# A fused attention kernel whose rotary query is turned by SBUF transfers instead of a second set of score products

## What is computed

```python
def _rotate_half(x):
    x1, x2 = jnp.split(x, 2, axis=-1)
    return jnp.concatenate([-x2, x1], axis=-1)
def _apply_rope(x, cos, sin):
    return x * cos[None, None] + _rotate_half(x) * sin[None, None]
...
h = _rmsnorm(hidden_states, ln1_w)
kv = _rmsnorm(kv_states, ln1_w)
q = (h @ Wq).reshape(bsz, q_len, NH, HD).transpose(0, 2, 1, 3)    # NH = 16, HD = 64
k = (kv @ Wk).reshape(bsz, k_len, NKV, HD).transpose(0, 2, 1, 3)  # NKV = 4
v = (kv @ Wv).reshape(bsz, k_len, NKV, HD).transpose(0, 2, 1, 3)
q = _apply_rope(q, cos_q, sin_q)
k = _apply_rope(k, cos_k, sin_k)
...
scores = jnp.einsum('bhqd,bhkd->bhqk', q, k) / math.sqrt(HD)
probs = jax.nn.softmax(scores + attention_mask, axis=-1)
attn = jnp.einsum('bhqk,bhkd->bhqd', probs, v) ... @ Wo
hidden = residual + attn
x = jax.nn.silu(x @ Wgate) * (x @ Wup) @ Wdown    # x = _rmsnorm(hidden, ln2_w)
```

## Time and profile before

| | us |
|---|---|
| median of 3 runs | 478.11 (475.93 to 478.21) |
| the profiled execution, its own time | 478.35 |
| its span | 476.5 |
| PE busy | 444.5 (93% of the span) |
| DVE busy | 373.0 (78%) |
| ACT busy | 297.7 (62%) |
| POOL busy | 272.9 (57%) |

### The profile page before, as it was taken

One profiled execution on the slowest core, in us unless ns is written; L12 is line 12 of the kernel. 1 busy time (PEld: TensorE's weight loads), 2 busy tenths in 40 slices (PEclk: granted clock), 3 DMA queues, 4 the chain that ended last, 5 costly groups with the idle time before them and its releaser, 6 DMA issues.

```text
span 476.5 us, 16997 instructions
## 1 busy us (share of the span) xinstructions
PE 444.5 (93%) x6888; PEld 352.7 (74%) x6888; DVE 373.0 (78%) x927; ACT 297.7 (62%) x726; POOL 272.9 (57%) x331
## 2 busy tenths in 40 slices
PE   5699999999999999999989888999999999999996
PEld 4367666767676776689878676798888888878776
DVE  5599888879898888968788987869687777868463
ACT  2377767768777877666873566565666657554351
POOL 6546796669978787965561556336453544541220
PEclk9799999999999999999999999999999999999999
DMA  8980000000000000000000000000000000000000
GB/s 289 229 276 3 2 3 1 3 3 1 3 4 3 1 4 2 3 1 2 1 1 3 2 1 3 2 12 3 12 3 1 14 3 13 1 14 3 14 1 22
DMA packets 12436, 11.54 MB, mean 24 GB/s; under 512 B 5192, under 2 KB 10312, under 8 KB 12360
## 3 DMA queue, kind: packets, MB, share of 16 engines
q1 hardware_dynamic: 11640, 9.01, 6.8%
q10 hardware_dynamic: 720, 1.45, 0.8%
HBM read 9.42 MB, written 1.05 MB: 22 GB/s over the span
## 4 chain that ended last, share of the span: by engine, by line
PE 66%; DVE 13%; issue 7%; ACT 6%; POOL 5%; DMA 1%; POOLq 0%; ACTq 0%; DVEq 0%
PE ps L474 7%; PE ps L456 5%; PE ps L488 5%; PE ps L626 5%; PE ps L766 5%; PE ps L642 5%; PE ps L664 4%; PE ps L464 3%; PE ps L540 2%; PE ps L553 2%; PE ps L619 2%; PE ps L414 2%; PE ps L634 2%; ACT shared L873 2%; PE ps L415 2%
## 5 line engine op out<-in xcount | busy, mean ns | idle before, releaser
L1355 DVE TENSOR_REDUCE negm<-ps 128x8 bf16<-128x512 f32 x96 | 59.6, 683 | 21.2 <-PE ps L456 21.2
L867 ACT ACTIVATE p<-ps 128x512 f32<-128x512 f32 x96 | 57.1, 598 | 25.8 <-PE ps L464 24.5
L873 ACT ACTIVATE shared<-ps 128x512 f32<-128x512 f32 x96 | 55.1, 604 | 20.1 <-PE ps L474 20.1
L474 PE MATMUL ps<-cst,p 128*128 128x128 f32 x384 | 61.2, 282 | 2.5 <-ACT p L867 0.6
L474 PEld LDWEIGHTS ps<-cst,p 128*128 128x128 f32 x384 | 42.3, 141 | 25.9 <-ACT p L867 14.9
L1902 POOL TENSOR_TENSOR wide<-wide,cv 128x1024 f32<-128x1024 f32 x24 | 45.7, 1903 | 26.1 <-ACT wide L857 26.1
L1955 POOL TENSOR_TENSOR probs<-p,rc 128x512 f32<-128x512 f32 x32 | 33.5, 1057 | 44.8 <-DVE rc L1664 44.8
L1829 POOL TENSOR_TENSOR rstd<-veps,neghalf 128x2 f32<-128x2 f32 x40 | 28.9, 722 | 46.8 <-DVE veps L1391 29.6
L626 PE MATMUL ps<-shared,wq 128*128 128x256 f32 x128 | 32.6, 399 | 3.5 <-ACT shared L1027 1.6
L464 PE MATMUL ps<-negm,idb 128*128 128x512 bf16 x96 | 32.8, 382 | 2.5 <-DVE negm L1355 2.3
L1081 ACT ACTIVATE late<-ps 128x512 f32<-128x512 f32 x32 | 17.3, 593 | 25.5 <-PE ps L789 25.5
(11 more groups left out here) (222 smaller groups left out, 1149.5 us busy)
## 6 DMA issues: line engine op xcount, KB each, us to landing
late<-in_mask_l SPq DMA_DIRECT2D x2, 512.0 KB, 10.5
result<-x_all SPq DMA_DIRECT2D x7, 128.0 KB, 1.8
x_all<-in_x_tok SPq DMA_DIRECT2D x1, 768.0 KB, 6.5
wide<-in_ctx_t SPq DMA_DIRECT2D x1, 768.0 KB, 7.9
rv<-in_rv ACTq DMA_DIRECT2D x1, 768.0 KB, 8.3
wa<-in_wa SPq DMA_DIRECT2D x1, 512.0 KB, 8.3
w<-in_w SPq DMA_DIRECT2D x2, 256.0 KB, 6.2
wq<-in_wq SPq DMA_DIRECT2D x1, 512.0 KB, 7.4
```

The lines of the kernel that those rows point to most:

```text
L474: ins = nc.tensor.transpose(bank[:, c * 128:c * 128 + 128], p3[:, n % 3, c * 128:c * 128 + 128], ident)
L867: A_(p3[:, n % 3, :], ps[:, S_BANK[r], :], ACT.Exp, scale=SC8).then_inc(sm["act_exp"], 1)
L873: A_(pt[:, w % 2, r, :], pt_bank(RG * w + r), ACT.Copy).then_inc(sm["act_pt"], 1)
L1355: V.tensor_reduce(negm[:, n % 4, :], ps[:, S_BANK[r], :].rearrange("p (a k) -> p a k", k=S), AX.X, ALU.max, negate=True).then_inc(sm["dve_ ...
```

## The change

For groups 2 to 7 the query is rotated in full before the scores. DVE makes the sine product of a projected tile apart (`sine`, into `q_sin`, 512 elements) and the cosine product in place (`read_q`, 512 elements): two instructions in place of one. SP moves the sine products to the partitions of the other half of each head, 32 partitions at a time: a pair of tiles is four transfers of 32 partitions x 1024 floats (128 KB each), `swap_halves`. POOL adds what has come to the cosine product (`turn_q`, 128x512). The swapped key goes: no `kcs`, no `ks`, and `scores3` has 32 matmuls in place of 64. The order changes too: PE projects `q0`, `q1` before the transposes `t0`, `t1` and `q2`, `q3` right behind them, all in the first half; DVE works `sine` and the reads of the first pair ahead of `l2_gate`, those of the second at the start of the second half; `rotate_k` stands ahead of the read of `out`; POOL turns the first pair at the start of its second half and the second pair at its end.

```diff
             (("s0", 0), ("s1", 0), ("pv0", -1), ("pv1", -1), ("l_in", 2), ("md", -2), ("l_text", 2), ("k", 2), ("out", -1),
-             ("in", 1), ("l_gate", 2), ("t0", 0), ("t1", 0), ("q0", 1), ("q1", 1)),
-            (("s0", 0), ("s1", 0), ("pv0", -1), ("pv1", -1), ("m_in", -1), ("kt", 2), ("ks", 2), ("q2", 1), ("q3", 1),
-             ("out", -1), ("v", 2), ("mg0", -1), ("mu0", -1), ("l_back", 2), ("t0", 0), ("mg1", -1), ("mu1", -1), ("t1", 0)),
+             ("in", 1), ("l_gate", 2), ("q0", 1), ("q1", 1), ("t0", 0), ("t1", 0), ("q2", 1), ("q3", 1)),
+            (("s0", 0), ("s1", 0), ("pv0", -1), ("pv1", -1), ("m_in", -1), ("kt", 2),
+             ("v", 2), ("out", -1), ("mg0", -1), ("mu0", -1), ("l_back", 2), ("t0", 0), ("mg1", -1), ("mu1", -1), ("t1", 0)),
...
+            def swap_halves(g):
+                half = HD3 // 2
+                for a in range(2):
+                    eng.wait_ge(sm["q_sin"], 4 * (g - TURNED) + 2 * a + 2)
+                    if g > TURNED:
+                        eng.wait_ge(sm["q_rot"], 4 * (g - TURNED - 1) + 2 * a + 2)
+                    two = slice(2 * a, 2 * a + 2)
+                    for i in range(4):
+                        to, of = half * i, half * (i ^ 1)
+                        eng.dma_start(q_swap[to:to + half, two, :], q_sin[of:of + half, two, :])\
+                           .then_inc(sm[f"q_swap{a}"], 16)
...
+                    if u == 0 and g >= TURNED:
+                        pe.wait_ge(*released("kt", g))
+                        pe.wait_ge(sm["q_rot"], 4 * (g - TURNED) + 2 * a + 2)
...
-                    for c in range(2):
+                    for c in range(1 if g >= TURNED else 2):
...
+            def q_times(g, i, to, c):
+                tab = cst[:, C_ROPEQ + c * S:C_ROPEQ + c * S + S].unsqueeze(1).to_broadcast([128, 2 * GB, S])
+                return V.tensor_tensor(to, bank_of(f"q{i}", g).rearrange("p (b q) -> p b q", q=S), tab, ALU.mult)
...
+            def sine(g, a):
+                if g > TURNED:
+                    dve.wait_ge(sm[f"q_swap{a}"], 64 * (g - TURNED))
+                for i in range(2 * a, 2 * a + 2):
+                    dve.wait_ge(sm["p_use"], filled(f"q{i}", g))
+                    q_times(g, i, q_sin[:, i, :].rearrange("p (b q) -> p b q", q=S), 1).then_inc(sm["q_sin"], 1)
...
+                if r + 2 < NG:
+                    rotate_k(r + 2)
                 if 1 <= r < NG:
                     read("out", n - 1)
                     m_rms_mean(r - 1)
                 if r + 2 < NG:
                     l2_max(r + 2)
+                if r + 1 < NG:
+                    sine(r + 1, 0)
+                    read("q0", r + 1)
+                    read("q1", r + 1)
                 if r + 2 < NG:
-                    rotate_k(r + 2)
                     l2_gate(r + 2)
...
+            def turn_q(g, i):
+                pool.wait_ge(sm[f"q_swap{i // 2}"], 64 * (g - TURNED + 1))
+                pool.wait_ge(*released(f"q{i}", g))
+                P.tensor_tensor(q_rows(g, i), q_rows(g, i), q_swap[:, i, :].rearrange("p (b q) -> p b q", q=S), ALU.add)\
+                    .then_inc(sm["q_rot"], 1)
...
             def second_half(r):
+                if r + 1 < NG:
+                    turn_q(r + 1, 0)
+                    turn_q(r + 1, 1)
                 if r + 2 < NG:
                     l2_fuse(r + 2)
                 if r < NG:
                     probs3(4 * r + 2)
                     probs3(4 * r + 3)
+                if r + 1 < NG:
+                    turn_q(r + 1, 2)
+                    turn_q(r + 1, 3)
```

More of the change, by code:

```diff
@@ L64 @@
 KEPT = 3
+TURNED = 2
 def constants():
@@ L119, in build @@
                            (blocks[:, 1024:3072], q3x[:, :]))]
+        q3_turned = [t.rearrange("p (a m q) -> p a m q", a=2, m=4) for t in (wide[:, 0:2048], q3x[:, :])]
+        q_sin = shared[:, 0:2048].rearrange("p (i n) -> p i n", i=4)
+        q_swap = ctx_tok[:, :, :].rearrange("p (i m) d -> p i (m d)", i=4)
         kcs = sb("kcs", [128, TG, NK3])
@@ L267, in build @@
         SECOND = (
-            (("s0", 0), ("s1", 0), ("l_back", 1), ("pv0", -1), ("pv1", -1), ("l_in", 2), ("kt", 1), ("ks", 1), ("k", 2),
-             ("l_text", 2), ("out", -1), ("l_gate", 2), ("t0", 0), ("in", 1), ("t1", 0), ("q0", 1), ("q1", 1)),
+            (("s0", 0), ("s1", 0), ("l_back", 1), ("pv0", -1), ("pv1", -1), ("l_in", 2), ("kt", 1), ("k", 2),
+             ("l_text", 2), ("out", -1), ("l_gate", 2), ("t0", 0), ("in", 1), ("q0", 1), ("q1", 1), ("t1", 0), ("q2", 1), ("q3", 1)),
             HALVES[1],
@@ L306, in bank_of, with q_rows @@
             return ps[:, ring_bank(slot[what, i]), :]
+        def q_rows(g, i):
+            m = 2 * (i % 2)
+            return q3_turned[g % 2][:, i // 2, m:m + 2, :].rearrange("p m (b q) -> p (m b) q", q=S)
         def released(what, i):
@@ L765, in scores3 @@
                                         rows = slice(j * S, j * S + S)
-                                        ins = mm(banks[j][h * S:h * S + S, cols], q3[gs][a][rows, c, 2 * i + h, toks[b]],
-                                                 k3[rows, g % KEPT, c, a, toks[b]], start=False, stop=True, skip_group_check=True)
+                                        ins = mm(banks[j][h * S:h * S + S, cols], q[rows, 2 * i + h, toks[b]],
+                                                 k[rows, toks[b]], start=False, stop=True, skip_group_check=True)
                 ins.then_inc(sm["s3"], 1)
@@ L1115, in joining @@
                 read("kt", 2)
-                read("ks", 2)
                 exps3(5)
@@ L1182, in second_half @@
                 if r + 2 < NG:
-                    read("ks", r + 2)
                     read("v", r + 2)
@@ L1695, in joining @@
                 sum3(5)
+                rotate_k(3)
                 read("out", 1)
@@ L1698, in joining @@
                 l2_max(3)
-                rotate_k(3)
+                sine(2, 0)
+                read("q0", 2)
+                read("q1", 2)
                 l2_gate(3)
@@ L1732, in second_half @@
                 if r + 1 < NG:
-                    read("q0", r + 1)
-                    read("q1", r + 1)
+                    sine(r + 1, 1)
+                    read("q2", r + 1)
+                    read("q3", r + 1)
                 if live:
@@ L1741, in second_half @@
                     sum3(2 * n)
-                if r + 1 < NG:
-                    read("q2", r + 1)
-                if live:
                     sum3(2 * n + 1)
-                if r + 1 < NG:
-                    read("q3", r + 1)
                 if live:
@@ L1958, in probs3 @@
                     .then_inc(sm["s3n"], 1)
+            def turn_q(g, i):
[3 more added lines that the diff above has]
+                    .then_inc(sm["q_rot"], 1)
             def sum_k(g):
                 pool.wait_ge(sm["d_kc"], g + 1)
+                if g >= TURNED:
+                    P.tensor_tensor(kc[:, :, :], kc[:, :, :], ks[:, :, :], ALU.add).then_inc(sm["d_kr"], 1)
+                    return
                 if g >= 1:
```

20 lines of the change are left out of this document (12 added, 8 removed).

## The result

| | before | after |
|---|---|---|
| median of 14 runs each, us | 477.45 (475.93 to 478.39) | 475.40 (474.51 to 476.77) |
| span of the profiled execution | 476.5 | 474.5 |
| its own time | 478.35 | 476.41 |
| PE busy | 444.5 | 434.3 |
| POOL busy | 272.9 | 293.6 |

The ratio is 0.9959, with a 95% interval of 0.9947 to 0.9971: 2.05 us shorter, 0.4%. The forecast was 473.3, 4.8 us shorter. The direction and the range held, the size did not: what came is less than half of it.

The account below looks back on a forecast made before the run. PE bounds the kernel at 26.96 us a round; afterwards a DVE and POOL ring of 26.56 does. Rounds 2 to 5 give 1.6, the end 2.9 and about 0.5: 5.0 off 478.35, median 473.3, own range 467.5 to 477.

Parts of the forecast that it names:

- Round 1 ... I take it as even: First round with the load: losses and gains cancel, `md` of round 2 stays at 312.4, bounds -1.8 and +1.2 us.
- the end: Behind `md` of round 6: PE sets the pace again, three sine sets fewer save 2.9 us, covered waits perhaps 0.5 more.
- The ring: DVE and POOL work from one `l2_norm` to the next: 19.79 plus 6.77, 26.56 us a round, taking the pace from PE.
- PE's need of "24.6": PE's work in a full round after the change: 26.96 less 1.92 for sine scores and 0.44 for transposes.
- The other large term, 1.6 for rounds 2 to 5: Four full rounds, each going from 26.96 to 26.56 us, save 1.6 us.
- the low bound: `rotate_k` on DVE at its old 1.36 us instead of 2.37; the kernel would be 4 us faster than forecast.
- My low bound of 467.5: Whole kernel, fast end of the forecast's own range: `rotate_k` 4 us less, turns 1.8 less, round 1 1.8 less.
- The rule of the lock: DVE instructions with two SBUF inputs and GpSimd ones exclude each other for a whole instruction, so `rotate_k`'s new place costs time.
- The transfers: A pair's sine products moved by SP before POOL's turns: 3.7 us taken against 4.6 free, hence hidden.
- The estimate that I worked out from the Trainium skill: Time of a pair's transfers by the skill's port figures: 1.5 + 2.0 + 1.2 = 4.7 us, just at the edge.
- The rival: A pair's transfers come late and POOL stands for them: 2.6 us a round, 13 us in all, 486; chance 0.15.
- The rival of PE's pace: PE still sets the pace, the whole 14.1 us comes: 464.2; chance 0.17, shared with something between, 464 to 468.

Follow-up runs that it names:

- the last four versions: Kernel with round 1's key rotation in its old place, plus one or two turns on DVE, alone or with key projected first: 468.09, 468.98, 467.46, 467.20 us.

## Why the prediction was wrong, point by point

- **The step that failed first is "Round 1 ... I take it as even".** `md` of round 2 came 2.1 us later, 1.8 of them from round 1 itself, outside the bound of 1.2. I had named the products, the turns and the projections there, but put the moved `rotate_k` at nothing: in `joining` `out` is ready when the sums end, so the rotation delays it, and with it the squares, ACT's read of `in` and the projections of q. That is 1.26 us, and 1.66 more through PE's clock. Without the move round 1 gains 1.12, within my bounds.
- **The second is "the end", 2.9 and 0.5.** 1.75 came. The sets of scores are gone as reckoned; from `md` of round 7 (442.58, before 443.64) the gain is 0.94 for one set. But the half microsecond that I added for waits covered by the projections is the wrong way round: POOL's 0.92 are covered, and 0.66 for `in` and 0.92 ahead of `out` are bared, since `q2` and `q3` no longer stand there. 0.66 more is lost that way. The rest, 0.45, lies in four groups of matmuls that take longer from start to start than before: `md` 1.96 for 1.88, `out` 2.00 for 1.79 and 1.86 for 1.78, `q0` 1.80 for 1.73. Why they do is not shown.
- **The ring held.** Reckoned 26.56, measured 26.37; cutting its POOL part shortened it, and PE's need of "24.6" was met by 24.7 to 24.9 of busy time with the ring open. The other large term, 1.6 for rounds 2 to 5, came out as 2.35.
- **One piece was right by luck.** Adding up the round of the timelines above piece by piece, every piece is within 0.2 us of mine. But for `rotate_k` I had 2.37, all of it collision, and called 1.36 the low bound. Here its instructions took 1.80 and it waited 0.68 for ACT's read of `k`: 2.48 in all, of which a part that I didn't have. That wait goes back to PE, which projects `k` behind `l_text`; with `k` first, three rounds took 25.95 to 25.97. The ring thus passes through PE at this place. And the old place, which I thought could save 4 us, costs 4.6 on the ratio, about half of it through the one late pair. My low bound of 467.5 was also added up wrongly: with all three terms that I named it is 465.7. A ring is not only what one engine does in a row; where it stands for another, that one's chain is part of it.
- **The rule of the lock bore out, and more widely than I used it.** Each `l2_norm` instruction, with one SBUF input, took 1.29 us beside POOL's turns and 0.34 otherwise. The first instruction of `rotate_k`, with two, took 1.21 in place of 0.69. The Trainium skill, "SBUF — State Buffer", "SBUF: two separate sides", counts among the DVE instructions that exclude a GpSimd one, besides those with two SBUF inputs, those in a 2-port mode, and says that whoever comes second is blocked until the other's instruction is over. The 1.29 agree with that; which mode `l2_norm` is in, no run here shows.
- **The transfers were hidden**, though not as priced. In rounds 2 to 6 SP issued eight in 5.5 to 5.8 us, about 0.7 each and not 0.50, and 128 KB landed 2.3 after the issue and not 1.8: 4.2 in place of 3.7, against 4.8 free. The estimate that I worked out from the Trainium skill, "SBUF — State Buffer", "Door 1: The DMA port swizzle" (4.7), was too long by half a microsecond. The rival is not dead: single pairs at 5.4 to 5.5 us, over the reserve, were seen in three of the experiments' profiles, each with an instruction fetch in its midst.
- **The rival of PE's pace** needed a ring shorter by 1.9 us. The changed kernel doesn't have it; the last four versions come near it, by edits of their own.

So the sum had one term nearly right (1.6, measured 2.35) and two that were wrong by 2.1 and 1.65 us, both at the ends of the block and both the same way.

## What to carry to other kernels

When work is taken from the engine that sets the pace, write down the ring that takes its place over all engines, PE included, and then price the first and the last round apart: what is a filled wait in a full round can be a new delay in a ramp. Look at each long wait of PE twice, since it can cost again as much in slower matmuls behind it (2.81 us of waiting, and 1.66 more behind it). And when an engine is late with a short value that another stands for, give the waiting engine the work that holds it up, rather than changing the order of the two.

## What the runs showed of the hardware

- After 2.81 us without a matmul, eight matmuls took 3.57 us in place of 1.89, at a granted clock of 0.62; after waits of 1.17 and 0.59 close together, 3.54; after 0.93 and 0.59, 1.89. With five needless products in the first gap the projection took 1.99, and `md` came 1.66 us sooner in the trace.
- A DVE `TENSOR_SCALAR` of 128x128 from SBUF to SBUF takes 0.34 us, and 1.29 beside a POOL `TENSOR_TENSOR` of 1.25: one of POOL's instructions for one of DVE's, also when POOL has two in a row.
- From SBUF to SBUF, a pair's four transfers of 32 partitions are all there 4.2 us after the first issue at 128 KB each and 3.8 at 16 KB. In the three cases of 84 in which an instruction fetch of 16 KB began 3.0 to 3.2 us after the first issue, it was 5.4 to 5.5, at either size.
